# Attention with the heads of a group on two halves of TensorE's rows, ScalarE's queue for the maxima, and a first stage in four slots

## The reference

```python
qkv = x @ W_qkv.T + b_qkv
scores = einsum('bhqd,bhkd->bhqk', Q, K) / sqrt(8)
attn = softmax(scores + causal)            # causal: -inf above the diagonal
x = layernorm(x + einsum(attn, V) @ W_o.T + b_o)
x = layernorm(x + gated_mlp(x) + looked_up_experts(x))
```

## Time and profile before

| what | value |
|---|---|
| median of 3 runs | 854.17 us (850.57 to 854.17) |
| the profiled execution | 851.66 us |
| its span, first to last instruction | 850.1 us |
| PE, DVE, ACT, POOL busy | 87%, 80%, 67%, 50% |
| TensorE clock granted | mean 0.94 |
| DMA traffic | 67.06 MB |

### The profile page before, as it was taken

How to read it: one execution, slowest core, us unless ns; L and a number is a source line. 1 busy time by engine, 2 the same in 40 slices (tenths; PEclk the granted TensorE clock), 3 DMA queues, 4 the chain that set the end, 5 groups by cost and what they waited for, 6 DMA issues and landing times. The chain is left out here.

```text
span 850.1 us, 17568 instructions
## 1 busy us (share of the span) xinstructions
PE 738.5 (87%) x4345; PEld 330.1 (39%) x4345; DVE 684.0 (80%) x2289; ACT 567.2 (67%) x926; POOL 423.6 (50%) x468
## 2 busy tenths in 40 slices
PE   6659899999999999999999998687788788887755
PEld 3332233333333333333333332233546455555345
DVE  5769999898998998989989890166888888888883
ACT  4440267666766676667666778558879798897771
POOL 8655111221122112211221123358999999999984
PEclk9885599999999999999999999997999999999997
DMA  6768535345543553355335330201001101100000
GB/s 174 225 159 200 113 73 120 83 94 125 120 86 84 126 125 80 88 124 126 81 86 123 83 81 23 89 2 52 1 3 36 38 1 38 37 1 13 4 11 25
DMA packets 58955, 67.06 MB, mean 79 GB/s; under 512 B 15488, under 2 KB 33536, under 8 KB 58880
## 3 DMA queue, kind: packets, MB, share of 16 engines
q1 hardware_dynamic: 53120, 62.35, 31.2%
q10 hardware_dynamic: 5184, 2.36, 1.0%
q0 software_dynamic: 576, 1.57, 0.7%
HBM read 46.73 MB, written 19.53 MB: 78 GB/s over the span
## 5 line engine op out<-in xcount | busy, mean ns | idle before, releaser
L698 ACT ACTIVATE probs<-ps 128x384 f32<-128x384 f32 (+2 forms) x384 | 290.9, 809 | 172.8 <-PE ps L752 170.7
L669 POOL TENSOR_SCALAR_AFFINE_SELECT probs<-probs 128x256 f32<-128x256 f32 x256 | 103.0, 407 | 361.4 <-ACT probs L698 359.0
L720 PE MATMUL ps<-Kx,Qx 128*128 128x512 bf16 (+3 forms) x768 | 233.0, 348 | 15.3 <-DVE mx L812 9.7
L808 DVE CUSTOM_DVE_ANT_0 junk<-ps,tri 128x256 bf16<-128x256 f32 (+3 forms) x512 | 228.2, 487 | 22.3 <-PE ps L720 18.8
L752 PE MATMUL ps<-Qa,Ka 128*128 128x512 bf16 (+3 forms) x768 | 180.3, 329 | 3.5 <-ACT probs L698 2.9
L812 DVE TENSOR_REDUCE mx<-ps 128x1 f32<-128x512 f32 x256 | 162.1, 681 | 13.8 <-issue 7.3
L738 PE MATMUL ps<-probs,Vg 128*9 128x512 f32 (+3 forms) x1536 | 153.3, 488 | 0.3 <-POOL probs L669 0.3
L720 PEld LDWEIGHTS ps<-Kx,Qx 128*128 128x128 bf16 x768 | 69.6, 98 | 207.0 <-DVE mx L808 85.8
L967 POOL TENSOR_TENSOR S<-sim 128x1024 f32<-128x1024 f32 x64 | 120.7, 1910 | 10.5 <-ACT sim L1030 5.4
L1219 DVE SCALAR_TENSOR_TENSOR A<-S,T,ps 128x511 f32<-128x511 f32 x128 | 90.1, 741 | 11.3 <-ACT ps L1041 9.4
L1041 ACT ACTIVATE ps<-S,nb 128x512 f32<-128x512 f32 x128 | 82.9, 680 | 11.4 <-DVE A L1219 10.8
(11 more groups left out here) (115 smaller groups left out, 862.6 us busy)
## 6 DMA issues: line engine op xcount, KB each, us to landing
Qx<-q_scr SPq DMA_DIRECT2D x48, 192.0 KB
Kx<-k_scr SPq DMA_DIRECT2D x48, 192.0 KB
Qa<-q_scr SPq DMA_DIRECT2D x48, 192.0 KB
Ka<-k_scr SPq DMA_DIRECT2D x48, 192.0 KB
o_scr<-Os SPq DMA_DIRECT2D x32, 256.0 KB, 2.2
q_scr<-qs SPq DMA_DIRECT2D x34, 128.0 KB, 3.2
k_scr<-qs SPq DMA_DIRECT2D x18, 128.0 KB, 3.1
xin<-in_L_attn_x_dram ACTq DMA_DIRECT2D x8, 256.0 KB, 3.8
```

The source lines that it names most:

```text
L669: pool.affine_select(out=diag, in_=diag, compare_op=ALU.is_ge, fill=0.0, base=0, pattern=[[0, 2], [1, P]], channel_multiplier=-1).then_inc ...
L698: act.activation(probs[:, k % 2, hh, 0:width], ps[:, bank:bank + 2, :].rearrange("p a c -> p (a c)")[:, 0:width], ACT.Exp, scale=SM_SCALE) ...
L720: pe.matmul(ps[:, X_BANK + f % X_SLOTS, 0:c1 - c0], Qx[:, u, hh, P * i:P * (i + 1)], Kx[:, u, hh, c0:c1], start=True, stop=True).then_inc( ...
L808: dve.tensor_tensor_reduce(out=junk[:, f % 4, 0:w], in0=src, in1=tri[:, CHUNK - w:CHUNK], scale=1.0, scalar=-BIG, op0=ALU.add, op1=ALU.max ...
```

## The change

It changes the layout of operands, the order on PE, who issues three transfers, and the first stage.

- The four heads of a group lie as 2 halves (`a`) by 2 places (`pl`). An operand tensor holds half 0 in rows 0 to 63 and half 1 in rows 64 to 127. 64 rows hold eight of the nine part products (all but part 2 with part 2). That last one and the maxima stand in new operands `Ql` and `Kl` (rows 0 to 2 of a half: the maxima against ones; rows 3 to 10: part 2 with part 2), so a score step is now four matmuls over 64 rows each: two halves of `Qa`, then two halves of `Ql`. A max chunk is one matmul over 64 rows and leaves out the last product. A score step now takes one key tile for two heads.
- `q_scr` stores each part once; `load_parts` repeats rows with a source that is broadcast in its outermost place. Ten DMAs for each pair of operands take the place of six; `load_last` adds four for Ql and Kl.
- The maxima are stored with four DMAs and fetched with two. Store, fetch, and the load of Qx and Kx of group n+3 are issued from ACT's queue, ahead of the exponentials of steps 15, 20 and 22 of the 24 of a group.
- `probs` has four slots of one key tile each instead of two of two tiles; `GROUP_ORDER`, `AHEAD` (17) and `COPY_AT` are new.
- In the first stage `qs` has four slots, two stores of q a half fall away, loops are unrolled, and the bias columns come in four DMAs.

The core of the diff:

```diff
+PL = GH // 2
+ROWS = P // 2
+FULL = PARTS * DH
-AHEAD = 18
+AHEAD = 17
-GROUP_ORDER = "xpxxpxsxxsxxsxxsxppxxsxsxxpxxxsspxxsxsxppxxsxxsxxxxxsspxsxxsxpxxsxsxpxssxxxpsxsxxsxs"
+GROUP_ORDER = "pxxsxsxpxsxxpxxpssxxpsxxsxxxsxsxpxxsxsxpxsxpxxsxxsxxxsxxxsppxsxxsxpxxssxxpxxsxsxxssx"
+M_STORE_AT, M_FETCH_AT, X_LOAD_AT = 15, 20, 22
...
-        qs = operands.enter_context(nc.sbuf_tensor("qs", [P, 2, 2, PARTS, CHUNK], BF16))
-        Qx, Kx, Qa, Ka = [operands.enter_context(nc.sbuf_tensor(name, [P, 2, GH, SEQ], BF16))
+        qs = operands.enter_context(nc.sbuf_tensor("qs", [P, QS, 2, PARTS, CHUNK], BF16))
+        Qx, Kx, Qa, Ka, Ql, Kl = [operands.enter_context(nc.sbuf_tensor(name, [P, 2, PL, SEQ], BF16))
...
         def load_parts(eng, qdst, kdst, g, done):
-            rows = PARTS * DH
-            for r in range(PARTS):
-                src = q_scr[g, :, r:r + PARTS, :, :].rearrange("n h s d t -> (n s d) h t")
-                eng.dma_start(qdst[rows * r:rows * (r + 1), :, :], src).then_inc(done, 16)
-                eng.dma_start(kdst[rows * r:rows * (r + 1), :, :],
-                              k_scr[g].rearrange("n h s d t -> (n s d) h t")).then_inc(done, 16)
+            for a in range(2):
+                q, k = [dst[ROWS * a:ROWS * (a + 1)].rearrange("p j t -> p (j t)") for dst in (qdst, kdst)]
+                qsrc = q_scr[g, a].rearrange("n s d j t -> (n s d) (j t)")
+                eng.dma_start(q[0:2 * FULL], qsrc.unsqueeze(0).broadcast_to([2, FULL, PL * SEQ])).then_inc(done, 16)
+                eng.dma_start(q[2 * FULL:ROWS], qsrc[0:ROWS - 2 * FULL]).then_inc(done, 16)
+                for s in range(PARTS):
+                    ksrc = k_scr[g, a, s].rearrange("n d j t -> (n d) (j t)")
+                    times = PARTS if s < PARTS - 1 else PARTS - 1
+                    eng.dma_start(k[FULL * s:FULL * s + DH * times], ksrc.unsqueeze(0).broadcast_to(
+                        [times, DH, PL * SEQ])).then_inc(done, 16)
+        def load_last(eng, u, g, done):
+            for a in range(2):
+                for dst, scr in ((Ql, q_scr), (Kl, k_scr)):
+                    eng.dma_start(dst[ROWS * a + PARTS:ROWS * a + PARTS + DH, u, :, :].rearrange("p j t -> p (j t)"),
+                                  scr[g, a, PARTS - 1].rearrange("n d j t -> (n d) (j t)")).then_inc(done, 16)
-        STORES = 6
+        STORES = 4
...
                 def _(act):
+                            if e == M_STORE_AT and not (isinstance(n, int) and n + 1 >= GROUPS):
+                                m_store(act, n + 1, bass.ds(n + 1, 1))
+                            if e == M_FETCH_AT and not (isinstance(n, int) and n + 1 >= GROUPS):
+                                m_fetch(act, n + 1, 1 - u, bass.ds(n + 1, 1))
+                            if e == X_LOAD_AT and not (isinstance(n, int) and n + 3 >= GROUPS):
+                                load_next_max(act, n + 3, 1 - u)
...
                     def scores(n, u, e, load):
-                        for j, q0, w, off in UNITS[k][1]:
-                            bank = S_BANK + 2 * (e % 2) + off // CHUNK
-                            mm = pe.matmul(ps[:, bank, off % CHUNK:off % CHUNK + w], Ka[:, u, hh, P * j:P * (j + 1)],
-                                           Qa[:, u, hh, q0:q0 + w], start=True, stop=True)
+                        for q, k, first in ((Qa, Ka, True), (Ql, Kl, False)):
+                            for a in range(2):
+                                rows = slice(ROWS * a, ROWS * (a + 1))
+                                mm = pe.matmul(ps[:, S_BANK + 2 * (e % 2) + a, 0:w], k[rows, u, pl, P * j:P * (j + 1)],
+                                               q[rows, u, pl, q0:q0 + w], start=first, stop=not first)
```

More of the change, by code:

```diff
@@ L24 @@
 PARTS = 3
-SPLIT_ROWS = PARTS * PARTS * DH
-M_ROW = SPLIT_ROWS
+PL = GH // 2
+ROWS = P // 2
+FULL = PARTS * DH
 VW = DH + 1
@@ L39 @@
 FAR = 1.0e38
[L43 to L46, removed]
+KTILES = []
+for _half in range(2):
+    for _j in range(4 * _half + 4):
         _q0 = max(P * _j, CHUNK * _half)
[L48 to L59, removed]
+        KTILES.append((_half, _j, _q0, CHUNK * (_half + 1) - _q0))
+PPG = len(KTILES)
+HALF_PIECES = sum(_half == 0 for _half, _j, _q0, _w in KTILES)
+DIAG_TILES = [t for t, (_half, _j, _q0, _w) in enumerate(KTILES) if _j >= 4 * _half]
+SPG = PPG * PL
+MPG = len(DIAG_TILES) * PL
+PROB_SLOTS = 4
 MAXC = []
@@ L65 @@
     for _part, (_c0, _c1) in enumerate([(0, CHUNK), (CHUNK, _end)] if _end > CHUNK else [(0, _end)]):
-        for _hh in range(GH):
-            MAXC.append((_i, _part, _hh, _c0, _c1))
+        for _pl in range(PL):
+            for _a in range(2):
+                MAXC.append((_i, _part, PL * _a + _pl, _c0, _c1))
 CPG = len(MAXC)
-AHEAD = 18
-GROUP_ORDER = "xpxxpxsxxsxxsxxsxppxxsxsxxpxxxsspxxsxsxppxxsxxsxxxxxsspxsxxsxpxxsxsxpxssxxxpsxsxxsxs"
+AHEAD = 17
+GROUP_ORDER = "pxxsxsxpxsxxpxxpssxxpsxxsxxxsxsxpxxsxsxpxsxpxxsxxsxxxsxxxsppxsxxsxpxxssxxpxxsxsxxssx"
 CARRIED = 4
-COPY_AT = (12, 4)
+COPY_AT = (14, 3)
 X_SLOTS = 3
-VG_AT = 41
+VG_AT = 46
+M_STORE_AT, M_FETCH_AT, X_LOAD_AT = 15, 20, 22
 FREE = 2
+QS = 4
+X_LOADS, S_LOADS, M_LOADS = 10, 14, 2
 ONE = 1
@@ L204, in build @@
         p3_made = sem("p3_made")
-        qk_stored = [sem(f"qk_stored{u}") for u in range(2)]
-        p3_stored = [sem(f"p3_stored{u}") for u in range(2)]
+        qk_stored = [sem(f"qk_stored{u}") for u in range(QS)]
+        p3_stored = [sem(f"p3_stored{u}") for u in range(QS)]
         pads_made = sem("pads_made")
@@ L362, in _ @@
                                  allow_slow_non_contiguous=True).then_inc(wts_loaded, 16)
-                    with sp.Fori(0, BATCH - 1) as b:
+                    for b in range(BATCH - 1):
                         store_parts(sp, b)
                     for u in range(2):
-                        sp.wait_ge(qk_stored[u], STORES * 16 + ONE)
+                        sp.wait_ge(qk_stored[u], STORES * 16)
                         sp.wait_ge(p3_stored[u], 32)
-                    sp.wait_ge(pads_made, 2)
                     load_parts(sp, Qx[:, 0], Kx[:, 0], bass.ds(0, 1), xop_loaded[0])
@@ L491, in _ @@
                     turn(0, 0)
-                    with pe.Fori(0, BATCH - 1) as b:
+                    for b in range(BATCH - 1):
                         turn(b, 1)
@@ L557, in _ @@
                     copy_turned(0, 1)
-                    with dve.Fori(0, BATCH - 1) as b:
+                    for b in range(BATCH - 1):
                         for u in range(2):
@@ L580, in build, with m_store, m_fetch, load_next_max @@
             mT = sa("mT", [P, PARTS * 32], BF16)
+            def m_store(eng, g, reg):
+                eng.wait_ge(m_chain, M_STEPS * (g + 1))
+                for b in range(4):
+                    eng.dma_start(m_scr[reg, :, :, b, :].rearrange("n s c r -> (n c) s r"),
+                                  mT[32 * b:32 * (b + 1), :].rearrange("c (s r) -> c s r", s=PARTS)).then_inc(m_stored, 16)
+            def m_fetch(eng, g, u, reg):
+                eng.wait_ge(m_stored, 64 * (g + 1))
+                for a in range(2):
+                    eng.dma_start(Ql[ROWS * a:ROWS * a + PARTS, u, :, :].rearrange("s j t -> s (j t)"),
+                                  m_scr[reg, :, 16 * a:16 * (a + 1)].rearrange("n s c b r -> (n s) (c b r)")).then_inc(
+                        mrow_loaded[u], 16)
+            def load_next_max(eng, n, u):
+                eng.wait_ge(mx_read, CPG * (n - 1))
+                load_parts(eng, Qx[:, u], Kx[:, u], bass.ds(n, 1), xop_loaded[u])
             with nc.Block() as block:
@@ L703, in _ @@
-                    with act.Fori(1, GROUPS) as n:
-                        group(n)
+                    group(0, 0)
+                    group(1, 1)
+                    with act.Fori(1, GROUPS // 2 - 2) as i:
+                        for u in range(2):
+                            group(2 * i + u, u)
+                    for n in range(GROUPS - 4, GROUPS):
+                        group(n, n % 2)
                     copy_out(GROUPS - 1, 1)
```

237 lines of the change are left out of this document (116 added, 121 removed).

## The result

The changed kernel takes 1074.28 us (median of 4 runs, 1073.84 to 1075.04) against 853.45 (850.57 to 854.17) before: ratio 1.2601, 95% interval 1.2575 to 1.2626. The forecast was slower, at 1000 us, with a range of 850 to 1110. The direction, the mechanism named first and the range held; the size was short by 74 us.

The account below looks back on a forecast made before the run. DVE, coupled with PE, was taken to bound attention, with operand loads on few DMA engines bounding it after the change. 851.66 + 147 (loads) + 0 - 2 (tail) = 997, so 1000 us at the median; range 850 to 1110.

Parts of the forecast that it names:

- the mechanism named first: Forecast A: in attention, few DMA engines carry the operand loads, making the kernel slower; chance 0.68.
- The operand loads: Attention: outermost counts of 2 or 3 confine loads to few DMA engines; the busiest needs 35.1 us a group.
- ACT's issues: 16 DMA issues a group at 0.45 us on ACT's queue, 7.2 us, ten of them (4.5 us) ahead of exponential 22.
- so 0.5 us shows, up to 2 with the fetch: What of ACT's block of issues ahead of exponential 22 would delay PE after 4.0 us of ACT idle.
- The cover: 4.0 us of ACT idle, placed ahead of exponential 22, taken to hide most of the 4.5 us of issues.
- Timing exposure: Qx and Qa loads start together and stall PE: 35 to 44 us a group, taken as 40, +147 us over 13 groups.
- Row halves side by side: Score step on PE: the two row halves run concurrently, so scores keep 7.9 us a group; otherwise 7.9 more.
- Rival C: Score step: row halves don't run together, loads spread, PE needs 32.7 us a group; 905 to 935 us, chance 0.07.
- DVE's floor: Attention: DVE's work stays 26.1 us a group, so no group can go below that.
- The maxima's way: Group start: earlier store and fetch of maxima remove a 1 to 2 us stall; about zero net with ACT's issues.
- First stage: Four slots remove ACT's 18.1 us wait for stores, gaining 6 us; net near zero (-4 to +4) after first-load costs.
- The tail: Last two groups: few maxima left and PE's maxima cheaper, -2 us.

Follow-up runs that it names:

- experiment 3: The changed kernel with only the issue of the Qx and Kx loads moved from ACT's queue to SP; 960.36 us (one run).
- experiment 1: The changed kernel with operand rows reordered so that every load's source has outermost count 8, loads still from ACT; 965.92 us.
- the square: Four kernels, Qx and Kx loads from ACT or SP: 1074.3 and 960.4 us at outermost count 2 and 3, 965.9 and 856.1 at 8.
- experiment 2: The kernel of experiment 1 with the Qx and Kx loads issued from SP; 856.13 us.
- experiment 5: The changed kernel with q parts stored repeated in DRAM, so loads are plain with no broadcast, still from ACT; 925.46 us.
- experiment 11: The kernel of experiment 2 with DVE's attention loop written out; 838.14 us.
- experiment 7: The kernel of experiment 6 with DVE's attention loop written out; 825.74 us.
- experiment 12: The kernel of experiment 7 with each q part stored once and 16 plain loads a pair; 815.17 us.
- experiment 8: The kernel before the change with only DVE's attention loop written out; 840.83 us.
- experiment 10: The kernel of experiment 6 with the Qx and Kx load moved to the start of the next group, ahead of Qa and Ka; 840.93 us.
- experiment 6: The kernel of experiment 5 with the maxima's store and fetch and the Qx and Kx load all issued from SP; 868.35 us.
- experiment 9: The kernel of experiment 6 with the load of Qa and Ka waiting six steps longer; 866.21 us.
- experiment 4: The kernel of experiment 2 with score matmuls ordered half 0's two, then half 1's two; 857.12 us (one run).

## Why the prediction was right, and where it was short

**The operand loads: right.** The sum of 35.1 us a group for the first DMA engine is 35.0 in experiment 3. The outermost count decides how many engines carry a load: with 2 and 3, the DMA share lies at 0.06 to 0.29 in the stretches of after; with 8 it stands at 0.49 while loads run (experiment 1), and 104 to 108 us are gone. The Trainium skill's rule ("DMA: Bandwidth & Descriptors", "Rules for kernel authors") is borne out by this pair of kernels.

**ACT's issues: mis-sized, the step that failed.** In "so 0.5 us shows, up to 2 with the fetch" both figures should be 8.4 to 8.8 us a group, the 110 and 114 us of the square over the 13 groups whose ACT issues a load. Three things were wrong.

*The length of the block.* It is 7.7 us and not 4.5. The 0.45 us of the earlier trace rows are plain transfers at a quiet time; broadcast or three-dimensional loads cost 0.6 to 0.8 us on ACT and 0.69 on SP (experiment 2), and plain ones 0.31 (experiment 5).

*The cover.* The 4.0 us of the earlier trace rows do not stand "at that very place". ACT's timeline of before has them ahead of exponential 16 of a group (326.95 us); ahead of exponential 22 stand 2.03 us, and 1.68 a group later:

```profile
304.77 0.87 ACT L698 ACTIVATE probs<-ps 128x384 f32<-128x384 f32 x2 [2.03 <-PE ps L752]
...
326.95 3.44 ACT L698 ACTIVATE probs<-ps 128x896 f32<-128x896 f32 x4 [3.96 <-PE ps L752]
```

After the change PE goes on with other work for about as long: its stall is the block less 1.8 to 2.0 us in all three kernels that have a block (7.7 and 5.84 in after, 9.5 and 7.67 in experiment 1, 5.7 and 3.66 in experiment 5).

*The clock.* The 3.6 us at the lower level behind the stall add an estimated 1.8 us. 5.8 + 1.8 = 7.6; the last us of the 8.4 to 8.8 was not followed up.

Experiment 11 shows the same of the small transfers: 2.3 us of issues cost 1.4 of PE's. The Trainium skill calls the issue time "usually small relative to the DMA itself" ("DMA: Bandwidth & Descriptors", "Issuing engines are not separate DMA queues"). Here too the block is shorter than its transfers, which PE gets only at 439.45; it costs by its place, on an engine that PE waits for, and experiments 1 and 2 differ only in who issues the loads and when.

**Timing exposure: mis-sized too.** The forecast took 40 us a group for 13 groups, 35.1 for the loads and the rest as a mean between no exposure and all 9 us of it. From the first score of group 0 to that of group 13 the trace has 43.6 us a group against 28.9 before: 13 x (14.7 - 11.3) = 44.6 us of the shortfall. The same groups last 35.0 us in experiment 3, so the exposure is 8.6 us, and it goes with ACT's block: the two were one term. The last three groups, for which the forecast had no excess, take another 19.1 us, 12.7 of them in the group with the last stall on Kx (702.40). There are 14 such stalls in the stage and not 13. Left out altogether was the clock: behind both stalls of the group shown PE starts at 1.2 GHz, an estimated 3.5 us of its 43.0.

**Row halves side by side: right.** PE's timeline of after, a 512-column step:

```profile
388.34 0.41 PE L779 MATMUL ps<-Qa,Ka 64*128 64x512 bf16 x2
388.56 0.40 PE L779 MATMUL ps<-Ql,Kl 64*128 64x512 bf16 x2
388.78 0.54 PE L747 MATMUL ps<-Kx,Qx 64*128 64x256 bf16 x2
```

Four matmuls start within 388.78 - 388.34 = 0.44 us, as two did before. Rival C is out.

**DVE's floor: right.** 26.1 and 26.2 us a group in experiments 7 and 12 against the 26.1 that was read. DVE is busy for 25.2 of the 26.2 in experiment 12, so it isn't quite the whole bound.

**The maxima's way: wrong cause.** That PE's maxima resume late because SP stores the maxima only behind the loads was argued from the order of events in one group. The stall stands at every second group only (269.57 and 326.07), which a step made in every group can't cause; experiment 8 takes it away with the maxima's way as it was.

**First stage: half right.** ACT no longer waits for stores; its waits from 14 to 60 us are now led by

```profile
ACT qf L462 <- PE ps L496: 4.3, 7, 1.1
```

against 18.1 us on stores, and the first load is issued at 44.51 instead of 50.70, the 6 us forecast. But the first max chunk that reads it starts 23.5 us later and not 16.5:

```profile
68.04 1.03 PE L747 MATMUL ps<-Kx,Qx 64*128 64x512 bf16 x3 [18.43 <-DMA Kx<-k_scr]
```

The ten issues alone last until 52.97 us, and SP issues the ten of group 1 from 53.74, for the same few engines; no run separates the two. The first score is 12.6 us late where the sum had zero; with spread loads it comes at 91.6, 7.2 us before. The tail gave 1.1 of the 2 us. 44.6 + 19.1 + 12.6 + 0.9 = 77 us, which is the gap between the sum of 997 and this execution, within rounding. That the forecast came within 7% is in part luck: the exposure, which was a guess between two bounds, stood in for the block that was put at next to nothing.

## What to carry to other kernels

Count, for every transfer, the outermost count of its source, since it sets the number of DMA engines at work; a broadcast belongs inside that dimension. An engine that computes on the critical path should issue no block of transfers there: price an issue by its own shape (0.3 us plain, 0.7 broadcast), and take as cover only the idle time directly ahead of the instruction that the block delays, not the longest of the group. And where a stall returns at every pass of a loop, with nothing waited for, try the loop written out.

## What the runs showed of the hardware that was not expected

- DVE's jump back at the end of a loop of two groups costs 1.7 to 2.2 us with few loads under way, and 4.3 to 5.1 with many. One packet of the queue of instructions goes at each jump. With few loads it starts within 0.3 us of the gap's start (experiment 10: 375.11, gap from 375.32), with many 1.8 to 2.6 us into it (experiment 6: 395.24, gap from 392.96; experiment 9: 389.78, gap from 387.53, right behind a load packet that ends at 389.78). In all 18 jumps of the three kernels DVE resumes 1.9 to 2.6 us after that packet starts. So what the loads lengthen is the time until the packet goes; that it waits behind them on its DMA engine fits this, but no run shows that engine's order itself.
- Written out, the loop saved 12.6 us in the kernel before, 18.0 in experiment 11 and 42.6 in experiment 7, where the gap was longest: six gaps of 4.7 us are 28, and the clock behind them adds an estimated 8.
- Matmuls on different row halves may start out of program order in the records (experiment 4).
